# A decoder layer on one core: an output projection, a store and a routing step change their places in three engines' lists

## What is computed

```
x = x + self_attention(layernorm(x))       # 32 heads of 64, 8 key/value heads, rotary, causal, a sink per head
x = x + cross_attention(layernorm(x), ctx) # q, k, v are the rows themselves, cut into groups of 8 rows
x = x + experts(layernorm(x))              # 8 experts, the best one per token, plus a shared one
```

## Time and profile before

| | us |
|---|---|
| median of 3 runs | 1930.46 |
| lowest, highest | 1926.59, 1932.18 |
| the profiled execution | 1931.86 |
| its span, first to last instruction | 1930.0 |

### The profile page before, as it was taken

One profiled execution on the slowest core, in us unless ns is written; L12 is line 12 of the kernel. 1 busy time (PEld: TensorE's weight loads), 2 busy tenths in 40 slices (PEclk: granted clock), 3 DMA queues, 4 the chain that ended last, 5 costly groups with the idle time before them and its releaser, 6 DMA issues. The chain is left out here.

```text
span 1930.0 us, 45378 instructions
## 1 busy us (share of the span) xinstructions
PE 1736.0 (90%) x15440; PEld 1391.7 (72%) x15441; DVE 1176.0 (61%) x2269; ACT 820.4 (43%) x1575; POOL 840.1 (44%) x1302
## 2 busy tenths in 40 slices
PE   3999999999999999999699899999998588999997
PEld 2787787778778778777577677777775588966664
DVE  5766776676677677667377677777774333422221
ACT  3334443433433434343247666666666233311211
POOL 4544654555465455455234333444434311144443
PEclk9999999999999999999779899999999699999999
DMA  5011111111111111111244344444442265222221
GB/s 178 17 56 45 38 54 54 38 43 54 41 41 54 47 37 52 54 38 40 70 106 107 93 113 109 112 111 114 115 116 71 83 222 175 80 60 69 67 62 40
DMA packets 145343, 148.43 MB, mean 77 GB/s; under 512 B 26194, under 2 KB 139926, under 8 KB 143482
## 3 DMA queue, kind: packets, MB, share of 16 engines
q1 hardware_dynamic: 139514, 133.46, 24.4%
q0 software_dynamic: 5760, 14.06, 2.3%
HBM read 93.46 MB, written 54.11 MB: 76 GB/s over the span
## 5 line engine op out<-in xcount | busy, mean ns | idle before, releaser
L1149 DVE TENSOR_REDUCE xmax<-bankX 128x4 f32<-128x1024 f32 x256 | 310.1, 1217 | 120.1 <-PE bankX L1234 118.6
L1102 ACT ACTIVATE xe<-bankXT 128x512 f32<-128x512 f32 x512 | 292.0, 597 | 107.9 <-PE bankXT L1245 93.1
L1245 PE MATMUL bankXT<-stq,stk 98*128 98x256 f32 x1024 | 229.8, 310 | 19.2 <-DMA stq<-sh 11.5
L369 POOL TENSOR_TENSOR roped<-ropeC,ropeD 128x512 f32<-128x512 f32 x160 | 205.8, 1292 | 57.7 <-DVE ropeD L530 57.6
L557 DVE TENSOR_TENSOR oTl<-bankV,oTh 128x512 fp32r<-128x512 f32 x128 | 88.1, 688 | 199.5 <-ACT oTh L445 199.5
L1245 PEld LDWEIGHTS bankXT<-stq,stk 98*128 98x128 f32 x1024 | 157.1, 192 | 57.9 <-ACT xe L1102 35.0
L662 PE MATMUL bankQ<-wqh,xnTh 128*128 128x512 f32 x384 | 189.7, 494 | 0.0
L1234 PE MATMUL bankX<-stk,stq 96*128 96x256 f32 x1024 | 173.5, 294 | 13.7 <-DMA rw<-in_rw 11.1
L361 POOL TENSOR_TENSOR prob<-prob,rden 128x1024 f32<-128x1024 f32 x64 | 121.9, 1904 | 88.2 <-DVE rden L553 88.2
L1234 PEld LDWEIGHTS bankX<-stk,stq 96*128 96x128 f32 x1024 | 147.4, 199 | 16.6 <-DMA rw<-in_rw 11.3
L662 PE MATMUL bankQ<-wql,xnTh 128*128 128x512 f32 x384 | 152.7, 398 | 0.0
(11 more groups left out here) (196 smaller groups left out, 4045.8 us busy)
## 6 DMA issues: line engine op xcount, KB each, us to landing
stackk_d<-chl SPq DMA_DIRECT2D x96, 128.0 KB, 2.3
stackq_d<-q2hl SPq DMA_DIRECT2D x96, 128.0 KB, 2.3
stk<-stackk_d SPq DMA_DIRECT2D x32, 384.0 KB
stq<-stackq_d SPq DMA_DIRECT2D x128, 96.0 KB
wexp<-in_wexp SPq DMA_DIRECT2D x8, 1536.0 KB
x_d<-x SPq DMA_DIRECT2D x64, 128.0 KB, 1.9
xrden<-inv_d SPq DMA_DIRECT2D x64, 128.0 KB, 2.5
xin<-xg_d SPq DMA_DIRECT2D x40, 128.5 KB
```

Of the source, the lines that this page charges most:

```text
L369: nc.gpsimd.tensor_tensor(roped[c % 3][:], ropeC[c % 2][:], ropeD[c % 2][:], ALU.add).then_inc(s_rsum, 1)
L1102: nc.scalar.activation(xe[q][:].rearrange("p n m -> p (n m)"), bT[:, q % 2, :], ACT.Exp).then_inc(s_xe, 1)
L1149: nc.vector.tensor_reduce(xmax[tile[1] % 2][:, :, a:b + 1:b - a].rearrange("p m h -> p h m"), bS[:, 2 * (pr % 2):2 * (pr % 2) + 2, :].rear ...
L1245: ins = nc.tensor.matmul(bT[:, q % 2, n * D:(n + 1) * D], stk[p][0:98, hd // 4, n * P:(n + 1) * P], stq[p][0:98, hd, :], start=True, stop= ...
```

## The change

Three edits, each a change of place:

1. In self-attention, TensorE's `project_out(u, 0)` stands ahead of `turn_probs(u, 2)`, no longer behind it.
2. In cross-attention, SyncE's store of `x2` of tile y stands behind the rows of maxima and `inverses_in(z)`, no longer ahead of them.
3. In cross-attention, VectorE's `place(y)` stands ahead of `max_x(tile, 6)`, no longer behind it.

```diff
@@ attention, TensorE's body
                 if rear:
                     results(u, 1)
+                    project_out(u, 0)
                     turn_probs(u, 2)
-                    project_out(u, 0)
                 if front:
                     turn_qk(tile, 3)
@@ cross, SyncE's body
                 if four:
                     inverses_out(z)
-                if five:
-                    yp = y[1] % 2
-                    sp.wait_ge(s_x2, at(y) + 1)
-                    sp.dma_start(G.x2_d[bass.ds(at(y) * P, P), :], x2[yp][:]).then_inc(s_fst[yp], 16)
                 if two:
                     w = prev(tile, 1)
                     sp.wait_ge(s_shv, at(w) + 1)
...
                 if four:
                     inverses_in(z)
+                if five:
+                    yp = y[1] % 2
+                    sp.wait_ge(s_x2, at(y) + 1)
+                    sp.dma_start(G.x2_d[bass.ds(at(y) * P, P), :], x2[yp][:]).then_inc(s_fst[yp], 16)
                 if one:
@@ cross, VectorE's body
                 for r in range(STEPS):
+                    if five and r == 6:
+                        place(y, routing)
                     if one:
                         max_x(tile, r)
...
                     if five and r == 4:
                         choose(y, routing)
-                    if five and r == 6:
-                        place(y, routing)
                     if four and r == 7:
                         stats_of(z)
```

## The result

The changed kernel takes 1867.19 us (median of 4 runs, 1865.62 to 1871.08), the kernel before beside it on the same chip 1930.95. The ratio is 0.9667, with an interval of 0.9643 to 0.9691. The forecast was 1871.0 in a range of 1860 to 1892. The profiled execution took 1871.08 us against 1931.86, a difference of 60.8 where the sum of the prediction had 59.5. The total is met closely, in part by luck: one term of the sum was too large, two were too small, and the experts, which have no term in it, took longer in this execution.

The account below looks back on a forecast made before the run. TensorE, busy nine tenths and more in both attention stages, was taken as the bound. Gains of 35 + 12 + 10.5 + 2 = 59.5 us, from the median of 1930.46, gave 1871 us, range 1860 to 1892.

Parts of the forecast that it names:

- the 1.10 us a tile: Self-attention, edit 1: `results(u, 2)` starts at 520.99 instead of 522.09, giving 34.1 us over 31 tiles.
- Rival (b): Self-attention: the wait only changes its name, ScalarE starting the copy behind `evac_O(u, 1)`; 16 us instead of 35, 1890 us; chance 0.08.
- 0.43 us a tile: Cross-attention, edit 2: gain from the earlier `place`, times 28 tiles 12 us, bounds 6 and 16.3.
- 10.5 us of the 11.5: Cross-attention, edit 3: share of TensorE's waits for the rows of maxima expected to go; lower end 4 us.
- the most that the three edits can give back in waits that the profile names: TensorE's three waits where the edits act, 56.9, 16.3 and 11.5 us, in sum 84.7 us.
- The part on the queue: SyncE, edit 3: the store behind `inverses_in` costs nothing, since the sends hide its wait; later loads leave when they do now.
- 2 us taken: Cross-attention clock: some of three half-clock stretches may go with the waits before them; 2 us, bounds 0 and 6.8.
- (a): Cross-attention: gains go elsewhere, ScalarE's exponentials or the loads setting the tile's pace; 4 us left, 1891 us; chance 0.15.
- (c): Both stages: all half-clock stretches go and waits give their full sums, 35 + 16.3 + 11.5 + 6.8; 1861 us; chance 0.07.
- (d): Self-attention: slower, a late rest of group 0 makes the moved projection hold the transposes; 13 us lost, 1943 us; chance 0.02.
- (e): Cross-attention: edit 2 or 3 does nothing because another semaphore is last; counted inside (a), without its own chance.
- Would-show list: Signs expected in the changed kernel's trace: both attention stages' tile and turn times, TensorE's waits, order on VectorE and SyncE.

## Why the prediction was right, step by step

**Edit 1: right, and the sum 2.4 us too large.** The projection fitted the wait, the transposes kept their time, the copy and the 0.05 us behind it came out as read from the last tile: 1.34 us from transposes to results, forecast and measured. The term that was mis-sized is the 1.10 us a tile, with its reason that from there to the end of the tile "every step [...] follows TensorE and moves with it": the result matmuls take 0.97 instead of 0.86 us to the next group when the copy releases them, because their first weight load has lost its head start. So the tile gained 1.00, not 1.10, and the 31 tiles 31.0 us, not 34.1. The 0.97 doesn't need a named wait: with the projection split it is 0.97 and 0.96 as well, where the profile names none, so it belongs to the release by the copy and not to idle time on the matmul row. The last tile gained more than the 0.9 forecast, 1.9 us, and about half of that is luck: TensorE ran at the lower clock in it and was back at the full clock sooner (from `results(u, 2)` to `results(u, 3)` 2.81 us instead of 3.73). With 0.3 us lost at the start, the stage gained 32.6 instead of 35. Rival (b), a copy begun late, is out: ScalarE's copy starts at once, as its row in the changed kernel shows.
```profile
477.27 0.60 ACT L439 ACTIVATE probT<-bankP 128x512 f32<-128x512 f32 x1 [1.74 <-PE bankP L639]
```
It starts 0.03 us after the transposes' end at 476.58 + 0.66.

**Edit 2: right in its mechanism, 5 us too small.** `place` fits VectorE's idle time and `turn_ctx` follows at once. I took 0.43 us a tile; alone the edit gave 0.61 by the loop turn, 16.9 us in all, slightly over my upper bound of 16.3. The two timelines of TensorE above say which term was short. From the shifted scores at 1195.85 to `turn_ctx` the distance shrank by 0.71 us (0.95 to 0.24). Then the next shifted scores come 0.54 us after `turn_ctx` instead of 0.19: TensorE now waits there for ScalarE's exponentials (its weight load, 0.39 us), so 0.35 is given back and 0.36 is left. That is the loss that I expected at this place. But further on `turn_max` (L1224 on `xhl`) follows the scores before it after 0.23 us (1193.20 - 1192.97) instead of 0.46 (1199.47 - 1199.01), because GpSimd's split of the maxima comes sooner: 0.23 more. The prediction named this second part and gave it no size of its own; together they are 0.59, of which 0.55 are seen at `results_x`. What held the split was GpSimd's own queue. `send(y)` (L1036) stands ahead of it there and waited for `posx`, as its row in the kernel before shows:
```profile
1197.57 1.14 POOL L1036 DMA_INDIRECT xg_d<-xr,posx  x1 [2.64 <-DVE posx L1197]
```
The split followed at 1198.87, though maximum 7 had ended at 1196.67 + 1.23 = 1197.90. In the changed kernel the send is issued 3.59 us after the rank (1191.26) instead of 4.17. One tile of each turn gained 0.8 to 0.9 (rank to `results_x` 6.65 to 6.83 before, 5.9 after).

**Edit 3: right, 2.5 to 5 us too small.** I took 10.5 us of the 11.5 that the waits were called. Alone it gave 13.0 to 15.4, more than the whole of the named waits. The gap between issues was 1.00 us (mean 0.97 over the loop's tiles) and is 0.42 in all but the first tile of a turn: 0.49 a tile, 28 x 0.49 = 13.7. The named wait, 0.46, counts from the modelled end of the matmul before, which lies after the moment at which TensorE could have issued again. The same holds in self-attention: 1.68 us are named, while the prediction's own 517.8 to 519.65 is 1.85. The prediction's use of the sum of named waits as "the most that the three edits can give back in waits that the profile names" was thus no upper bound on the gain: this edit gave more than its share of it. The rows of the weight loads are closer here: in the kernel before they name 0.55 us at the shifted scores (the load at 1204.90; gained: 0.58) and 0.75 before `turn_ctx` (the load at 1196.80; gained there: 0.71). The part on the queue was right: the store behind `inverses_in` delayed nothing, since the sends hide its wait.

The late completions that the Trainium skill warns of (Perfetto Trace Analysis, section on DMA Instruction — HWDGE) do not show here: `inverses_in` is issued at 1196.35, just behind the sends at 1194.96 + 1.20 and 2.7 us after `inverses_out` at 1193.63.

**Clock: 2 us taken; not settled.** Before the last tiles of cross-attention the kernel before had three stretches of the lower clock, 6.8, 3.4 and 3.4 us long; the changed kernel had one of 3.4 us, and so had its repeat. The tiles with the three stretches took 19.80, 17.99 and 17.80 us, 7.3 us more in all than the same tiles of an undisturbed turn; in the changed kernel it is one tile of 17.25 us, 2.3 more. So about 5 us of the 32.2 came with disturbed tiles, their longer waits and the lower clock together, which is within the bounds of 0 and 6.8 but more than the 2 taken. It isn't shown to be the edits' doing: with the same cross-attention code as the kernel before, edit 1 alone had two such stretches. Of the rivals, (a) is out (the gains did not go elsewhere); (c), 1861, comes near because waits gave more than their full sums, and not because all half-clock stretches went; (d) did not come, since the transposes keep their time; (e) is out by the runs of edits 2 and 3 alone.

**The experts' 4.0 us more** are no part of the change. Their instructions are the same, and the clock of the stage differs by 0.01, which over 409 us is 4 us of clock. In all twelve traces, whatever the edits, the stage took between these two, 409.3 and 413.3 us; the kernel before happens to be the lowest and the changed kernel the highest, and the repeat of the changed kernel took 409.7. Without these 4 us the sum would have been 5 us short of the measured gain.

**Would-show list.** Tile 27.33 (27.2 forecast), wait before the transposes 0.16 (under 0.4), wait for `probT` 0.25 (about 0.3), no wait for `posx`, idle time split around `place`: all as said. The loop turn was 59.1, not 60.2, which is edits 2 and 3 being undersized. Two waits for rows of maxima were left where I had said none.

## What to carry to other kernels

A wait named on a matmul row is measured from the modelled end of the matmul before it; the gain from removing it is read better as the distance between issues, less the distance that the same two groups have where nothing waits. The wait on the row of the weight load came within 0.04 us of the gain in three places here (0.36 and 0.37, 0.55 and 0.58, 0.75 and 0.71; at the transposes of the kernel before it says 2.08 where the issues say 1.85), and it shows a wait where the matmul rows are busy without a gap. When work is put into a wait, time the whole chain from its head to the engine's next step: shifting more filler changed nothing, while putting the head of the chain half a projection sooner gave 10 us. And before an instruction is moved ahead of another in an engine's queue, compare the arrival of its input with the arrival of the other's: one step sooner turned a gain of 17 us into a loss of 25 against the better place.

## What the runs showed of the hardware

**The clock fell after short waits, but not after all of them.** Before the last tiles of cross-attention the twelve traces have twelve stretches of the lower clock. Nine begin within 2.5 us after a wait for the rows of maxima (0.62 to 1.73 us), one after a wait for `posx` (0.64, edit 1 alone) and two after waits for a maximum (0.55 and 0.56, `place` ahead of maximum 5). Six kernels or repeats have none there, those with edit 3 alone and with edits 2 and 3 among them. In the last tiles every kernel has the lower clock, and in the repeat of the changed kernel a stretch begins there with no named wait longer than 0.26 us in the 8 us before it. The stretch in the changed kernel follows a wait for the rows of maxima. SyncE's issues there:
```profile
1341.33 2.54 SPq L910 DMA_DIRECT2D inv_d<-xiden  x2
```
TensorE's timeline behind them:
```profile
1346.75 0.50 PE L1245 MATMUL bankXT<-stq,stk 98*128 98x256 f32 x2 [0.87 <-DMA stq<-sh]
```
And windows around it:
```profile
1346.00:1354.00 8.00, 7.25 (x60) 4.84 (x60) 4.35 (x14) 3.60 (x8) 3.54 (x5) 0.79 0.74 181
```
A wait of 0.87 us, then 2 x 0.21 x 8 = 3.4 us at 1.2 GHz. Waits just as long had no fall behind them: 0.94 us with edits 2 and 3 alone, four of 0.78 to 0.90 us with edit 2 alone, 1.06 us in the kernel before. That the wait causes the fall is argued, not shown, and stays open.

**An issue on SyncE sometimes takes twice its time.** The two DMAs of `inverses_out` above took 2.54 us to issue, in the tile shown first 1.28 (issue at 1193.63). This is what brought one of the two waits that were left. No run shows what holds the queue there.

**A group of matmuls that a semaphore releases late** costs about 0.1 us more than the same group behind other work (0.97 against 0.86 us here), because its first weight load can't run 0.11 us ahead under the work in front of it. It does so also where the matmul rows show no idle time.
